# A per-tile lead, moved slots in the first chunk, and a last chunk closed block by block

## What is computed

```python
u, res = split(x @ W_in)                      # 512 inner channels each
u = silu(causal_conv3(u, W_conv))
dt, B, C = split(u @ W_x)                     # 16 + 16 + 16
delta = softplus(dt @ W_dt + b_dt)
for each state n of 16, along the tokens:
    h = exp(delta * A[n]) * h + (delta * u) * B[n]
    y += h * C[n]
y = (y + u * D_param) * silu(res)
x = layernorm(x + y @ W_out)
logits = x @ router_w.T                       # top 2 of 8, then expert lists and experts
```

## Time and profile before

| what | us |
|---|---|
| median of 3 runs | 2411.4 (2409.33 to 2412.35) |
| the profiled execution | 2411.18 |
| its span, first to last instruction | 2409.1 |
| first scan of chunk 0 | 37.31 |
| start of routing | 1598.17 |
| busy: PE / DVE / POOL / ACT | 2249.4 / 2156.7 / 1826.8 / 1746.1 |

### The profile page before, as it was taken

One profiled execution on the slowest core, in us unless ns is written; L12 is line 12 of the kernel. 1 busy time (PEld: TensorE's weight loads), 2 busy tenths in 40 slices (PEclk: granted clock), 3 DMA queues, 4 the chain that ended last, 5 costly groups with the idle time before them and its releaser, 6 DMA issues. The chain is left out here.

```text
span 2409.1 us, 39456 instructions
## 1 busy us (share of the span) xinstructions
PE 2249.4 (93%) x14163; PEld 1809.6 (75%) x14163; DVE 2156.7 (90%) x2928; ACT 1746.1 (72%) x2928; POOL 1826.8 (76%) x1008
## 2 busy tenths in 40 slices
PE   8899999999999999999999997744999999999995
PEld 4577777777777777777777776633999999999995
DVE  6899999999999999999999999986787787787775
ACT  4889999899899998998998998842344344334355
POOL 3699999999999999999999999823336436437465
PEclk9999999999999999999999999975999999999998
DMA  3212212212212222222222211112122322322353
GB/s 104 69 55 71 79 63 80 71 62 71 88 63 80 77 65 71 79 72 70 71 71 80 71 62 62 62 70 74 32 67 40 88 66 44 85 66 45 89 196 136
DMA packets 88354, 178.91 MB, mean 74 GB/s; under 512 B 9041, under 2 KB 51281, under 8 KB 88161
## 3 DMA queue, kind: packets, MB, share of 16 engines
q1 hardware_dynamic: 73280, 154.11, 19.3%
q0 software_dynamic: 14880, 22.29, 5.1%
HBM read 140.20 MB, written 36.18 MB: 73 GB/s over the span
## 5 line engine op out<-in xcount | busy, mean ns | idle before, releaser
L554 POOL TENSOR_TENSOR dbu<-du,b_all 128x2048 f32<-128x2048 f32 x255 | 1159.3, 4548 | 59.6 <-DVE dbu L838 33.3
L946 DVE TENSOR_TENSOR_SCAN hst<-da,dbu 128x512 f32<-128x512 f32 x1008 | 1172.0, 1204 | 19.5 <-ACT da L694 16.0
L694 ACT ACTIVATE da<-delta,a_neg 128x512 f32<-128x512 f32 x1008 | 693.3, 698 | 100.8 <-DVE hst L946 97.1
L2233 PE MATMUL gu<-x_part,w_part 128*128 128x384 f32 (+1 forms) x2304 | 485.5, 359 | 3.1 <-DVE x_part L1980 1.7
L2233 PEld LDWEIGHTS gu<-x_part,w_part 128*128 128x128 f32 x2304 | 402.6, 188 | 34.2 <-issue 4.5
L1109 PEld LDWEIGHTS hd<-ident,hst 128*128 128x128 f32 x2048 | 242.1, 142 | 180.9 <-issue 121.3
L664 ACT ACTIVATE hTC<-w,c_tok 128x512 f32<-128x512 f32 x512 | 351.1, 686 | 21.7 <-PE w L1109 19.6
L1027 PE MATMUL gen<-xT,w_u 128*128 128x512 f32 x720 | 360.6, 599 | 4.3 <-ACT u_raw L626 4.3
L1109 PEld LDWEIGHTS w<-ident,hst 128*128 128x128 f32 x2048 | 244.7, 141 | 142.2 <-issue 101.5
L860 DVE SCALAR_TENSOR_TENSOR yacc<-hd,c_tok,yacc 128x512 f32<-128x512 f32 x458 | 333.7, 729 | 14.3 <-PE hd L1109 10.4
L1109 PE MATMUL hd<-ident,hst 128*128 128x128 f32 x2048 | 314.9, 277 | 33.5 <-DVE yacc L860 26.1
(11 more groups left out here) (323 smaller groups left out, 2796.1 us busy)
## 6 DMA issues: line engine op xcount, KB each, us to landing
b_all<-b_rows SPq DMA_DIRECT2D x128, 512.0 KB, 3.7
xT<-in_xT SPq DMA_DIRECT2D x16, 514.0 KB, 5.0
xT_r<-in_xT SPq DMA_DIRECT2D x16, 512.0 KB, 5.1
x_rows<-in_x SPq DMA_DIRECT2D x16, 512.0 KB, 3.8
x_dram<-x SPq DMA_DIRECT2D x16, 512.0 KB, 3.0
acc_dram<-x SPq DMA_DIRECT2D x16, 512.0 KB, 4.5
w_raw<-in_wg SPq DMA_DIRECT2D x8, 1024.0 KB, 5.0
w_raw<-in_wu SPq DMA_DIRECT2D x8, 1024.0 KB, 7.3
```

Of the source, the lines that this page charges most:

```text
L554: nc.gpsimd.tensor_tensor(dbu[DBU[n]][:], du[parity][:], b_n, ALU.mult).then_inc(dbu_ready, 1)
L694: nc.scalar.activation(da_bank[t % 2][:], delta[parity][:, t, :], ACT.Exp, scale=a_neg[:, t, n:n + 1]).then_inc(da_ready, 1)
L946: nc.vector.tensor_tensor_scan(hst[DBU[n]][:, t, :], decay[:], dbu[DBU[n]][:, t, :], 0.0, ALU.mult, ALU.add).then_inc(scanned, 1)
L2233: last = nc.tensor.matmul(gu_bank[n % 2][i][:, 0:width(n)], gu_part[wp][:, i, kk, f * P:(f + 1) * P], x_part[xp][:, kk, tokens_of(j)], sta ...
```

## The change

At the start: make_ident's block is gone, its two instructions stand at the head of POOL's program. SP issues xT first, then W_in in two halves, and the broadcast of W_convT after the small weights. PE runs 10 products of ident by ident (WARM) before it waits for data. ACT preloads the silu table. diag_d and the tap products are made by POOL. Softplus, du and dbu of state 0 go tile by tile, woven into the slots 0 to 3 of chunk 0; the relu of tiles 2 and 3 is on ACT; dbu of state 1 is made by POOL in four instructions. The slots of chunk 0 are dealt anew; in all chunks u0's first part goes from slot 26 to 24 and its fifth from 32 to 33, cT from 26 to 27 (read at 28), d3 from 37 to 38.

At the end: the 17th stage is replaced by `finish()` on each engine, which takes the blocks of 128 tokens one at a time in the order 0, 2, 1, 3. DVE gates straight from PSUM; ACT computes the inverse root as exp(-0.5 * ln(var + eps)); DVE normalises; the stores go block by block. The choice of experts is made for 56 tiles, its wide steps on POOL: three at state 13 of chunk 15, the rest after it; DVE makes the reductions (two of them in slots 32 and 56 of chunk 15), ACT the Exp in slot 57. Routing makes the choice for 8 tiles instead of 4.

```diff
-    "cT": (0, 26), "u0": (1, 26, 29, 30, 32, 34, 34), "d0": (0, 28), "d1": (0, 32), "d2": (0, 35),
-    "u1": (1, 36, 39, 39, 40, 41, 43), "d3": (0, 37), ...
+    "cT": (0, 27), "u0": (1, 24, 29, 30, 32, 33, 34), "d0": (0, 28), "d1": (0, 32), "d2": (0, 35),
+    "u1": (1, 36, 39, 39, 40, 41, 43), "d3": (0, 38), ...
...
+LAST_ORDER = (0, 2, 1, 3)
+EARLY_TILES = (CHUNKS - 2) * LT
+TOP_AT, TOP_EXP_AT, TOP_MAX_AT = 13, 57, (32, 56)
...
+    "v0": (0, 0, 0, 0, 1, 1, 2), "v1": (1, 0, 0, 2, 2, 3, 3), "v2": (0, 2, 2, 3, 3, 3, 3),
+    "v3": (1, 4, 4, 5, 5, 8, 10), "r0": (0, 7, 8), "r1": (0, 10, 12), "r2": (1, 14, 14), "r3": (0, 15, 16),
...
+    "r0": 10, "r1": 13, "r2": 15, "r3": 18, "xd": 27, "cT": 33, "u0": 30, ..., "v0": 1, "v1": 2, "v2": 7, "v3": 13,
```

SP and the head of PE:

```diff
-            sp.dma_start(w_staging, w_in_d[:, :, 0:DI]).then_inc(w_loaded, 16)
             sp.dma_start(xT[:], xT_d[:, :, 0:CL + 2]).then_inc(xt_loaded, 16)
...
+            for i in range(2):
+                cols = slice(i * (DI // 2), (i + 1) * (DI // 2))
+                sp.dma_start(w_staging[:, :, cols], w_in_d[:, :, cols]).then_inc(w_loaded[i], 16)
...
+            for i in range(WARM):
+                nc.tensor.matmul(gen_bank[1][:, 0:P], ident[:], ident[:], start=True, stop=True)
```

ACT in the first four slots of chunk 0, and DVE's part of a tile:

```diff
+                        if n == 0 and not s.close:
+                            if t < DT - 1:
+                                lead_size(t + 1)
+                            act.wait_ge(lead_delta, t + 1)
...
+                        if n == 0 and not s.close:
+                            if t < DT - 1:
+                                lead_soft(t + 1)
+                            if t == 0:
+                                lead_ud(0)
+                            if t == DT - 1:
+                                lead_ud(1)
...
+            def lead_terms(t):
...
+                dve.wait_ge(lead_soft_step, 2 * t + 2)
+                ins = nc.vector.tensor_tensor(delta[0][:, t, :], delta[0][:, t, :], tmp[:, t, :], ALU.add
+                                              ).then_inc(lead_delta, 1)
...
+                nc.vector.tensor_tensor(du[0][:, t, :], delta[0][:, t, :], u[:, t, :], ALU.mult
...
+                nc.vector.tensor_tensor(dbu[DBU[0]][:, t, :], du[0][:, t, :], b_all[0][:, 0, :], ALU.mult
```

The end, DVE's scaling and loop over the blocks, and the order on PE:

```diff
+                def scale_rows(m):
...
+                    v.tensor_scalar(x1[:, l, :], resid[:, l, :], mean_var[:, l, 0:1], rstd[:, l:l + 1],
+                                    ALU.subtract, ALU.mult).then_inc(x1_ready, 1)
...
+                for m, l in enumerate(LAST_ORDER):
+                    dve.wait_ge(last_projected, m + 1)
+                    v.tensor_tensor(resid[:, l, :], last_bank[l][:, 0:DM], x_rows[:, l, :], ALU.add
...
+                    v.bn_stats(stats[:, l, :], resid[:, l, :]).then_inc(last_row_step, 1)
...
+                    v.bn_aggr(mean_var[:, l, :], stats[:, l, :]).then_inc(last_row_step, 1)
+                    if m:
+                        scale_rows(m - 1)
...
+                for m in range(LT - 1):
+                    project(m)
+                flip(0)
+                project(LT - 1)
+                flip(1)
+                for m in range(2, LT):
+                    score(m - 2)
+                    flip(m)
+                score(LT - 2)
+                score(LT - 1)
```

More of the change, by code:

```diff
@@ L484, in _ @@
             pool.wait_ge(consts_set, N_CONSTS)
+            pool.wait_ge(ident_step, 2)
+            pool.wait_ge(weights_in, N_WEIGHTS * 16)
+            for t in range(DT):
+                nc.gpsimd.tensor_scalar(diag_d[:, t, :], ident[:], d_par[:, t:t + 1], None, ALU.mult
+                                        ).then_inc(diag_ready, 1)
+            for i in range(2):
+                pool.wait_ge(w_loaded[i], 16)
+            pool.wait_ge(spread_loaded, 16)
+            for tap in range(N_TAPS):
+                nc.gpsimd.tensor_tensor(w_u[:, tap, :, :], w_staging, gate[:, tap:tap + 1, :].to_broadcast([P, KD, DI]),
+                                        ALU.mult).then_inc(taps_ready, 1)
             def chunk(s):
@@ new lines, in link, with same @@
+            def link(*several):
+                for ins in several:
+                    steps[0] += 1
+                    ins.then_inc(top_step, 1)
+                pool.wait_ge(top_step, steps[0])
+            scores = logits[:, 0:EARLY * NE].rearrange("p (t e) -> p t e", e=NE)
+            full = [P, EARLY, NE]
+            first_wins = k["first_wins"][:].to_broadcast(full)
+            g = nc.gpsimd
+            def same(out, wide, top):
+                link(g.tensor_tensor(out, wide, top.to_broadcast(full), ALU.subtract))
+                link(g.tensor_scalar(out, out, 0.0, None, ALU.is_equal))
@@ L753, in chunk @@
                         nc.scalar.activation(first_da[:], first_arg[:], ACT.Exp).then_inc(first_decay, 1)
-                    if slot in NORM_AT and s.close and not s.last:
+                    if slot in NORM_AT and s.close:
                         l = NORM_AT.index(slot)
@@ L834, in _ @@
-            dve.wait_ge(b_loaded[0], 16)
-            for h in range(2):
-                half = slice(h * (DT // 2), (h + 1) * (DT // 2))
-                dve.wait_ge(lead_du if h == 0 else du_ready, 1)
-                ins = nc.vector.tensor_tensor(dbu[DBU[0]][:, half, :], du[0][:, half, :], b_all[0][:, 0:1, :].to_broadcast(
-                    [P, DT // 2, CL]), ALU.mult)
-            ins.then_inc(dbu_ready, 1)
-            def add_state(s, state, l):
+                if t not in RELU_ON_ACT:
+                    dve.wait_ge(lead_abs, t + 1)
+                    nc.vector.tensor_scalar(delta[0][:, t, :], lead_bank[f"d{t}"][:], b_dt[:, t:t + 1], 0.0, ALU.add,
+                                            ALU.max).then_inc(lead_relu, 1)
@@ L844, in add_state @@
+            def add_state(s, state, l, bank=hd_bank):
                 index, n, parity = state
@@ L955, in chunk @@
                             add_state(s, s.state_before(n, 1), 0)
-                        if s.close and not s.last:
+                        if s.close:
                             sum_rows(s, "o0")
@@ L1017, in fill @@
                 parts = len(s.fill_at[name]) - 1
-                if part == 0 and not (name == "C1" and s.last):
+                if part == 0:
                     s.wait_bank(pe, name, ring_read, rows_summed, scanned)
@@ L1049, in fill @@
                 elif what == "C":
-                    held = list(STASH[c - 1].items()) if j == 1 and not s.last else []
+                    held = list(STASH[c - 1].items()) if j == 1 else []
                     if part == 0:
@@ L1059, in fill @@
                         last = nc.tensor.matmul(bank[:, t * P:(t + 1) * P], rows[:, t, :], ident[:],
[L1060 removed]
+                                                start=part == 0 and t == 0,
                                                 stop=part == parts - 1, is_transpose=True, skip_group_check=True)
```

473 lines of the change are left out of this document (291 added, 182 removed), and 9 rows, old and new, of tables (FILL_AT, FIRST_FILL_AT).

## The result

The changed kernel takes 2394.4 us (median of four runs, 2392.7 to 2394.8), the kernel before 2411.1 beside it: a ratio of 0.9932, with a 95% interval of 0.9916 to 0.9947. That is 16.7 us less. The profiled execution took 2394.69 us with a span of 2392.8, so the span fell by 16.3. "Joined kernel" is the changed kernel from here on.

The account below looks back on a forecast made before the run. VectorE was taken to set the steady pace, leaving gains at the lead and the closing, a chain of waits. Terms -9.8 + 0.3 + 1.3 - 5.5 + 0.4 = -13.3 from 2411.4 give 2398 us, range 2392 to 2405.

Parts of the forecast that it names:

- rivals A: Whole kernel: the sum of the forecast's terms holds, 2398 us (2394 to 2402); chance 0.58.
- Rival C: Chunk 0: slots 4 to 19 at the steady 1.36 us and the clock up early, -17, 2394; chance 0.13.
- Step 1: Lead: without make_ident's block and with W_in halved, first data arrives at 5.2 to 6.0 us.
- Step 2: Lead: warm-up passes before data; first real matmul at 6.0 us, clock rise about 7.7, e0 full at 9.0.
- Rival F: Lead: the warm-up does not raise the clock in time, chunk 0 as now, 2405 to 2408; chance 0.03.
- Steps 3 and 4: Lead: ScalarE's table loaded early, e0's eviction ends at 9.7 us; diag_d and taps on GpSimd, done near 19, hidden.
- Step 5: Lead: convolution starts about 9.75 us, xdT there about 19.0, 4.3 earlier (3.2 without the clock, 5.2 at best).
- Step 6: Chunk 0 from xdT to silu: tile-by-tile chain, slot 8 at 46.7 us, silu at 65.6; lead and front -9.8.
- Rival B: Chunk 0 goes on as now, tile chain longer by a late v0; front -5, total -8.5, 2403; chance 0.16.
- Step 7: Other slots of chunk 0: the moves give 0, within 1.5 us either way.
- Rival E: Steady chunks: u0's moved part holds the turns in each of 14 chunks; at 1.3 us each, 2416; chance 0.02.
- Rival D: Closing: port conflict holds four scalings up to 1.0 us each behind GpSimd's steps; +4, 2402; chance 0.08.

Follow-up runs that it names:

- e0: Not a run: a tile TensorE fills in the lead and ScalarE evicts; forecast full at 9.0 us, its eviction of 0.70 ending at 9.7.
- no_warm: Joined kernel with WARM set from 10 to 0, so no warm-up passes; first eight passes 6.50 us, xdT copied at 20.35, gate's activation at 68.67.
- filler: Joined kernel plus fourteen identity passes on TensorE in the gaps of slots 18 and 19 of chunk 0; ratio 0.9932 (0.9915 to 0.9948).
- pieces_early: Joined kernel with GpSimd making each piece of dbu of state 1 right behind VectorE's own; slot 8 at 44.46 us, gate's activation at 65.54 instead of 65.74.
- light_early: pieces_early without four of the six parts of chunk 0's v3 fill (3.4 us of TensorE's work); slot 14 at 53.52 us, gate's activation at 63.62.
- first_old: Joined kernel with chunk 0's own slots put back as before, v0 and v1 read after slots 3 and 4; 2399.0 us, silu at 68.16.
- close_only: The new closing alone on the lead and all slots of the kernel before; 2407.0 us, ratio 0.9981 (0.9972 to 0.9991).

## Why the prediction was right, and where its terms were off

The forecast was 2398 (2392 to 2405), faster by more than 0.2% with 0.92; measured 2394.4. It was right, 3.6 us too careful, and at the edge between rivals A and C. By the table above the terms were too careful by 4.0 us in five stretches and too hopeful by 1.0 in two, so the total is nearer than its parts by some luck. Point by point:

- **Step 1, the first transfers.** Data forecast at 5.2 to 6.0; W_in's half arrived at 6.1. Right within 0.1.
- **Step 2, the warm-up, was mis-sized.** I let the clock rise 6 us after TensorE's first activity, so that e0 still ran slowly and the passes were worth 1.1 us. In the joined kernel it had risen within the warm-up, about 3 us after the start, and no_warm puts the warm-up's worth at 2.9. In filler it rose only with the second real pass, at 7.2 us, near the 7.7 that I had; so part of the 0.9 is this execution's fortune. This is the 0.9 us by which xdT came early, and the rest of the chain kept it. Rival F was wrong. The Trainium skill (TensorE: Matmul & The Clock Gate, Part 1: The HAM clock gate) describes a 1.2 GHz default from which sustained activity releases the engine, with an onset that varies from run to run; the passes at 0.84 and 0.46 fit its two levels, and the 3.67, 3.73 and 4.08 us of the same eight passes fit the varying onset.
- **Steps 3 and 4.** GpSimd's taps ended at 19.3 (forecast near 19), the v fills began at 23.0. Hidden, as said.
- **Step 5.** xdT at 18.1 (17.41 + 0.68) instead of 19.0; between the bounds.
- **Step 6, the slots.** First scan 25.2 (forecast 26.0), v0 read at 30.4 (31.5), v1 at 35.6 (36.8), the fourth scan's end 38.1 (39.2), slot 8 at 45.9 (46.7). All are 0.8 to 1.2 under the forecast, the lead's 0.9: the chain through ScalarE's queue was right. From slot 8 on I took TensorE's sum of work, 18.2, rounded up to 19; from slot 8 to the silu it took 18.0. pieces_early and light_early show that TensorE's list is indeed what ends last there, and first_old that the moved reads of v0 and v1 are what fills it. Rival B was that chunk 0 goes on as before; it did not. Rival C's 2394 is the measured time, but by other means: slots 4 to 19 took 1.62 us each and not 1.36 (37.98 to 63.92), and its "clock up early" is the part that was true.
- **Step 7, the rest of chunk 0.** +0.5 measured, 0 forecast. The 0.5 is a fall of the clock worth 1.4, which this execution had, less 0.9: without the fall it is 94.8 against 95.6 before. The kernel before has a fall of its own in its silu (0.54 between 75.4 and 79.0). first_old, with the old slots of chunk 0 and no fall there, takes 95.2; so about 0.45 are the slots' and the other 0.4 go with the fall of the kernel before, as far as one execution of each can say.
- **The steady slots** were weighed wrongly. I argued that VectorE had nothing to win, and that u0's part ahead of two turns could cost up to 0.3 a chunk. They give 0.08 a chunk. The sum of the waits in the earlier trace rows doesn't show where: they are the same after (4.0 and 4.1 us). The comparison slot by slot shows it, behind slot 37; which of the moved entries gives it stays open. Rival E, slower by this very move, had the sign wrong.
- **The last chunk.** Two reductions of 0.61 and 0.63 us, 1.2 in all, cost 0.7. The first puts the scans back by 0.5, of which 0.35 are made up within four slots; the second puts them back by 0.5, and of that nothing is made up.
- **The closing.** -5.8 against -5.5: right for the reason given, with stages as forecast relative to the last scan (projection at +5.4, forecast 5.6; last x1 ready at +15.4, forecast 14.8 (1588.3 - 1573.5)). Those 0.6 are the hold of the last scaling; from there to the routing I had given 4.4 and it took 3.5.
- **Rival D was right as a mechanism and wrong in size.** Four scalings held by up to 1.0 each would have made 4 us; in the joined kernel only the last was held by more than 0.1, for 0.6. There the last scaling ends at 1577.56 and GpSimd's step at 1577.41; the third ends at 1576.33 and GpSimd's step at 1576.18. pieces_early, with the same instructions in the closing, fell out otherwise: its scalings take 0.79, 0.80, 1.06 and 0.40. Its second, with the step that it meets:

```profile
1572.97 0.96 POOL L667 TENSOR_TENSOR delta<-du 128x448 f32<-128x448 f32 x1
1573.29 0.80 DVE L1048 TENSOR_SCALAR x<-resid,row_mean_var,rstd 128x256 f32<-128x256 f32 x1
```

  This one and the third end 0.16 and 0.15 us after GpSimd's step. By the rule that I quoted (the Trainium skill, SBUF — State Buffer, Who interferes with whom) the later one waits for the whole of the other. These four cases agree. The first scaling of pieces_early does not: it takes 0.79 and ends 0.63 us before the GpSimd step that began 0.09 after it (L639, 1571.30 to 1572.63). By the rule that step would have waited for the scaling, but it took the 1.33 that it takes alone; here the measurement speaks against the rule, and why the scaling is long stays open. The three long scalings put the end of the last only 0.1 later (15.53 after the last scan against 15.43), so the stage has room for holds ahead of the last. What counts is not the number of held scalings, by which rival D reckoned, but whether the last is held. The hold is long only where GpSimd's step has just begun.
- **The routing's choice** cost 0.9 instead of 0.4. The forecast's own factors, 18 steps by 32 columns by 0.001 us, make 0.6 and not 0.4. The rest is two of its steps: L1532 and L1533 took 0.55 and 0.48 where their neighbours take 0.22. In close_only the same two took 0.40 and 0.32. In all twelve executions with the new choice both end within 0.03 us of the end of GpSimd's iota into slot_high (joined: 1583.84 and 1583.81), while with the old choice the first of them starts 0.1 us ahead of that iota and takes 0.18. That the iota holds them is thus likely, and no experiment tested it.

## What to carry to other kernels

When a stall is removed at a pipeline's front, write down for each engine the sum of the work that lies ahead of the next landmark: here TensorE's list had become the longest, and 1.45 us won on GpSimd bought 0.2 us. Cut one profiled execution at landmarks that every variant has, and compare stretches: this gave 0.1 to 0.2 us where the times gave 4, provided that a fall of the clock, in the stretch or just ahead of it, is recognised by the clock column. Where a stretch differs, compare it slot by slot: that found the two reductions in the last chunk. In a short serial stretch, look at what GpSimd starts just ahead of the last step on VectorE: held steps further ahead cost 0.1 us here, the last one 0.6.

## What the hardware showed that I had not expected

- The clock fell behind the same 6 us of half-busy TensorE (3.10 of 6.00 us) in some executions of the same stream of instructions and not in others; a fall cost 1.4 us of the chunk.
- Twenty small passes (128 columns each, 3.96 us) ahead of the first data saved 2.9 us of a lead of 25. In the eleven executions that have them they took 3.96 to 4.64, and the saving at xdT was 2.3 to 3.0.
- The clock column read 1.00 over a lead in which eight passes took 6.50 to 6.75 us instead of 3.67: the trace's clock records begin only with the first rise (13.84 us in the kernel before). In the start of a kernel the duration of a pass is the better witness.
- From the last scaling's end to the routing's start, where the last wait is SyncE's for a 128 KB store, the executions take 2.6 to 3.8 us.
